# Adding attention's residual in TensorE's accumulator, and copying the sum with ScalarE

## The chip, the cores and the metric

The kernel runs on one core of one Trainium2 chip. The metric is device time in microseconds (us), the median of several runs. One more execution is recorded by the hardware profiler; its time and its span stand in the table below. The engines are TensorE (PE in the rows, PEld for its weight loads), VectorE (DVE), ScalarE (ACT), GpSimd (POOL) and SyncE (SP, which only issues transfers here). Each engine has its own list of instructions and works it off in order; engines meet through semaphores only.

## The reference

Sixteen sequences of 256 tokens with 128 features pass through half a mixture-of-experts block, an attention block, and half a mixture-of-experts block again. What the change touches is the middle line:

```
x = x + 0.5 * ffn(layernorm(x))
x = x + attn(layernorm(x))
x = x + 0.5 * ffn(layernorm(x))

def attn(x):                      # x here is layernorm(x), "xn" in the kernel
    q, k, v = split(einsum(rms_norm(x), w_qkv))
    q, k = rms_norm(q), rms_norm(k)
    w = exp(k); kv = w * v
    y = sigmoid(q) * cumsum(kv) / (cumsum(w) + 1e-6)
    u, g = split(einsum(y, w_swiglu))
    return x + einsum(u * silu(g), w_out)
```

So attention's new x is the old x, plus its layernorm xn, plus the projection of u * silu(g) with w_out.

## The kernel before

Tokens lie on 128 partitions; a tile is 128 tokens, X holds all 32 tiles in SBUF as [128, 32, 128] in fp32. The first and the last third of the time are the two mixture-of-experts layers (l = 0 and l = 1). Between them, from about 299 to 419 us, lies the attention stage, and the change lies wholly in it.

Attention works on one sequence at a time (two tiles, TB = 2; 16 sequences, BATCHES). It is cut into small stages, and each engine runs a software pipeline over them that is written out in full: in step k it runs, for each stage in the order of its list (POOL_STAGES, DVE_STAGES, ACT_STAGES, PE_STAGES), the stage for sequence k - lag, where the lag is the number beside the stage's name. Step k runs from 0 to 24. A stage begins with its waits on semaphores; an engine that waits there runs nothing of what stands behind.

One sequence goes through these stages (engine, lag; the names of the tiles are those of the rows):

- add_routed (POOL, 1): adds two loaded tiles Y to X. at_statistics and at_aggregate (DVE, 2 and 3), at_rsqrt and mean_square (POOL, 3 and 4), at_normalise (DVE, 4): the layernorm, written to xn.
- transpose_xn (PE, 4) into psT, copy_anT (ACT, 4) to anT, qkv (PE, 4) into psG or psH, squares (ACT, 4), qkv_rsqrt (POOL, 5: at_ms, then at_fac), weights (ACT, 5: wkv by Exp, tq by Tanh), weigh_v (DVE, 5).
- cumulate (PE, 6) into psU: three matmuls, of which the first and the third are lines 1643 and 1645. denominator (ACT, 6: den), invert, scale_q and attend (DVE, 6: rec, ysc, ya).
- transpose_y (PE, 7) into psT, copy_yT (ACT, 7) to yT, swiglu (PE, 7) into psU, tanh_g (ACT, 8: tg), gate_g and gate_u (DVE, 8: ag, ha).
- project (PE, 9) into psY, add_attention (DVE, 9): X = X + 0.5 * psY.
- residual (POOL, 5): X = X + xn, ahead of add_attention.

Waits that matter below: cumulate waits for attend of the sequence before it; transpose_xn waits for the copy_yT of the same step, since both use the psum tile psT; project waits for gate_u, and for the addition of the sequence before it to have read psY; gate_g waits for tanh_g.

From step 16 on, VectorE also begins the next layer's layernorm (stats and normalise, lines 761 to 774) of the chunks of four tiles that are done; LN_STEPS says in which step. From step 20 on, TensorE also transposes and scores these chunks (turn_chunk, score_chunk) at the head of a step.

Of the kernel before, what the change touches and what calls it, by code (L numbers as in the profile page):

```python
# [13 lines left out]
P = 128  # L14
D = 128
# [6 lines left out]
CH = 4  # L22
# [3 lines left out]
TB = SEQ // P  # L26
# [13 lines left out]
RING = 3  # L40
SEND_LAG = RING + 2
BATCH = 4
DEEP = 4
BATCHES_P = TOPK * TILES // BATCH
ROW = D + TOPK
# [24 lines left out]
SUM_LAG = 1  # L70

POOL_STAGES = [("qkv_rsqrt", 5), ("residual", 5), ("at_rsqrt", 3), ("mean_square", 4), ("add_routed", 1)]
DVE_STAGES = [("at_normalise", 4), ("at_aggregate", 3), ("gate_g", 8), ("at_statistics", 2), ("gate_u", 8),
              ("invert", 6), ("scale_q", 6), ("weigh_v", 5), ("attend", 6), ("add_attention", 9)]
ACT_STAGES = [("tanh_g", 8), ("denominator", 6), ("copy_yT", 7), ("copy_anT", 4),
              ("weights", 5), ("squares", 4)]
PE_STAGES = [("cumulate", 6), ("transpose_y", 7), ("project", 9), ("transpose_xn", 4), ("qkv", 4),
             ("swiglu", 7)]
# [1 line left out]

LN_STEPS = {}
for c in range(CHUNKS - 1):
    added = CH // TB * (c + 1) + dict(DVE_STAGES)["add_attention"]
# [11 lines left out]
fp32 = mybir.dt.float32  # L96
# [3 lines left out]
ALU = mybir.AluOpType  # L100
ACT = mybir.ActivationFunctionType
# [65 lines left out]
def macaron(nc, x, w_qkvT, w_swigluT, w_outT, gateT, w1_e, w3_e, w2_e, w1_s, w3_s, w2_s, out):  # L167
    ctx = ExitStack()
    with ctx:
# [6 lines left out]
        def sem(name):  # L176
            return ctx.enter_context(nc.semaphore(name))
# [6 lines left out]
        def overlaid(*groups):  # L184
# [7 lines left out]
            for name, shape, dt in groups[-1]:  # L192
# [3 lines left out]
        X = sb("X", [P, TILES, D])  # L196
# [13 lines left out]
        WOUT = sb("WOUT", [P, D])  # L210

        ident = sb("ident", [P, P])
# [47 lines left out]
        at_mv = sb("at_mv", [P, 2, TB, 2])  # L260
# [55 lines left out]
        pair = memory["pair"]  # L316

        memory = overlaid(
            [("xn", [P, 2, TB, D], fp32),
             ("anT", [P, 2, TB * P], fp32),  # L320
             ("sq", [P, 2, TB, D], bf16),
             ("wkv", [P, 2, TB, 2, D], fp32),
# [17 lines left out]
        xn = memory["xn"]  # L340
# [11 lines left out]
        ha = memory["ha"]  # L352
# [9 lines left out]
        psT = ps("psT", [P, 512])  # L362
        psY = ps("psY", [P, 512])
# [5 lines left out]
        attn_in = sem("attn_in")  # L369
# [71 lines left out]
        xres_done = sem("xres_done")  # L441
        anT_psum = sem("anT_psum")
        anT_done = sem("anT_done")
        qkv_psum = sem("qkv_psum")
# [14 lines left out]
        ha_done = sem("ha_done")  # L459
        at_psum = sem("at_psum")  # L460
        at_added = sem("at_added")

        psQKV = [psG, psH]
# [115 lines left out]
        def _(pool):  # L580
# [51 lines left out]
            for l in range(2):  # L632
# [77 lines left out]
                def residual(s):  # L710

                    wait_apart(pool, xn_ready, s.i + 1)
                    xs = X[:, bass.ds(s.i * TB, TB), :]
                    pool.tensor_tensor(xs, xs, xn[:, s.u % 2, :, :], ALU.add).then_inc(xres_done, 1)

                def qkv_rsqrt(s):

                    pool.wait_ge(ss_done, s.i + 1)
# [8 lines left out]
                                       .rearrange("p (a t) -> p a t", a=3), ALU.pow).then_inc(qk_scaled, 1)  # L727

                if l == 0:
                    stages = {"qkv_rsqrt": qkv_rsqrt, "add_routed": add_routed, "residual": residual,  # L730
                              "at_rsqrt": at_rsqrt, "mean_square": mean_square}
# [12 lines left out]
        def _(dve):  # L744
# [34 lines left out]
            for l in range(2):  # L779
# [332 lines left out]
                def at_normalise(s):  # L1112

                    dve.wait_ge(at_scaled, s.i + 1)
                    if s.past(2):
                        dve.wait_ge(anT_psum, s.i - 1)
                        dve.wait_ge(xres_done, s.i - 1)
                    for t in range(TB):
                        xt = X[:, bass.ds(s.i * TB + t, 1), :].rearrange("p a d -> p (a d)")
                        i = dve.tensor_scalar(xn[:, s.u, t, :], xt, at_mv[:, s.u, t, 0:1],  # L1120
                                              at_rstd[:, s.u, t:t + 1], ALU.subtract, ALU.mult)
                    i.then_inc(xn_ready, 1)

# [37 lines left out]
                    dve.tensor_tensor(ha[:, s.u, :], ag[:, s.u, :], psU[:, 1, 0:256], ALU.mult)\  # L1161
                       .then_inc(ha_done, 1)

                def add_attention(s):
                    dve.wait_ge(at_psum, s.i + 1)
                    dve.wait_ge(xres_done, s.i + 1)
                    xs = X[:, bass.ds(s.i * TB, TB), :].rearrange("p t d -> p (t d)")
                    dve.scalar_tensor_tensor(xs, psY[:, 0:TB * D], 0.5, xs, ALU.mult, ALU.add)\
                       .then_inc(at_added, 1)

                stages = {"weigh_v": weigh_v, "gate_u": gate_u, "add_attention": add_attention,
                          "at_normalise": at_normalise, "at_statistics": at_statistics, "attend": attend,
                          "at_aggregate": at_aggregate, "invert": invert, "scale_q": scale_q, "gate_g": gate_g}

# [13 lines left out]
        def _(act):  # L1188
            act.wait_ge(consts, CONSTS)
            for l in range(2):  # L1190
# [116 lines left out]
                if l == 1:  # L1307
                    continue

                def copy_anT(s):  # L1310
                    act.wait_ge(anT_psum, s.i + 1)
                    if s.past(2):
                        act.wait_ge(qkv_psum, s.i - 1)
                    act.activation(anT[:, s.u % 2, :], psT[:, 0:TB * P], ACT.Copy).then_inc(anT_done, 1)
# [44 lines left out]
                stages = {"copy_yT": copy_yT, "tanh_g": tanh_g, "weights": weights, "copy_anT": copy_anT,  # L1359
                          "squares": squares, "denominator": denominator}  # L1360
                def copy_turned(c):

# [25 lines left out]
        def _(pe):  # L1388
# [19 lines left out]
            for l in range(2):  # L1408
# [23 lines left out]
                for c in range(TURNED if l else 0, CHUNKS + 1):  # L1432
                    if c < CHUNKS:
# [5 lines left out]
                        for t in range(CH):  # L1439
                            i = pe.transpose(psH[:, c % 2, t * P:(t + 1) * P], XN[:, c * CH + t, 0:D], ident[:, :])  # L1440
# [176 lines left out]
                def transpose_xn(s):  # L1617
                    pe.wait_ge(xn_ready, s.i + 1)
                    issued = s.i + ((1 if y_first else 0) - apart)
                    if not isinstance(issued, int) or issued > 0:  # L1620
                        pe.wait_ge(yT_done, issued)
                    if s.past(1):
                        pe.wait_ge(anT_done, s.i)
                    for t in range(TB):
                        i = pe.transpose(psT[:, t * P:(t + 1) * P], xn[:, s.u, t, :], ident[:, :])
                    i.then_inc(anT_psum, 1)

                def qkv(s):
# [41 lines left out]
                def project(s):  # L1670
                    pe.wait_ge(ha_done, s.i + 1)
                    if s.past(1):
                        pe.wait_ge(at_added, s.i)
                    for t in range(TB):
                        i = pe.matmul(psY[:, t * D:(t + 1) * D], ha[:, s.u, t * P:(t + 1) * P], WOUT[:, :],
                                      start=True, stop=True)
                    i.then_inc(at_psum, 1)

                stages = {"project": project, "transpose_y": transpose_y, "swiglu": swiglu, "cumulate": cumulate,
# [70 lines left out]
```

## Time and profile before

| | |
|---|---|
| time, median of 3 runs | 709.31 us (708.37 to 711.33) |
| the profiled execution | 708.63 us, its span 706.9 us |
| busy over the span | PE 632.6, DVE 440.8, POOL 401.6, ACT 375.0 us |
| attention stage | about 299 to 419 us |

The span is the time from the first to the last instruction; 1.7 us lie around it. Busy shares over the whole span say little, since attention is a stage of its own with its own limits: it has to be read from stretches, and within a stretch from the order of instructions on each engine. A timeline row reads: start, length, engine, line, operation, out<-in, tile shape, and how many instructions were merged into it (x2); in brackets, how long the engine sat idle before, and which instruction of another engine ended that. An fp32 matmul shows as two records, a transpose as one, so project's two matmuls are "x4".

### The profile page before, as it was taken

All of it is one profiled execution on the core that took longest, in us unless ns stands there. A gap on an engine that the chain in (4) does not pass through costs nothing.

```text
span 706.9 us, 13752 instructions
## 1 busy us (share of the span) xinstructions
PE 632.6 (89%) x4622; PEld 572.5 (81%) x4622; DVE 440.8 (62%) x1167; ACT 375.0 (53%) x819; POOL 401.6 (57%) x485
## 2 busy tenths in 40 slices
PE   3877998999999999858886777899999999999995
PEld 2656888999999999725664574788999999999983
DVE  6679785555445553359999876975545554455336
ACT  2657725666666652146664536572666666665220
POOL 5610065677777773479987416005577777777330
PEclk9999999999999999979999997799999999999999
DMA  9634011223332121221100000701222332222137
GB/s 295 251 63 60 1 32 43 72 84 86 111 83 51 53 53 62 87 75 45 46 16 1 0 1 1 122 0 32 47 75 82 111 84 81 54 53 54 57 125 260
DMA packets 38820, 51.38 MB, mean 73 GB/s; under 512 B 6432, under 2 KB 27936, under 8 KB 38368
## 3 DMA queue, kind: packets, MB, share of 16 engines
q1 hardware_dynamic: 29664, 31.73, 15.5%
q0 software_dynamic: 9088, 18.78, 10.3%
q8 instruction: 39, 0.64, 0.4%
q14 instruction: 29, 0.24, 0.1%
HBM read 34.81 MB, written 15.66 MB: 71 GB/s over the span
## 4 chain that ended last, share of the span: by engine, by line
PE 64%; DVE 20%; issue 4%; POOL 4%; ACT 4%; DMA 3%; SPq 1%; POOLq 0%; ACTq 0%; DVEq 0%
PE psY L1573 17%; PE psU L1394 5%; PE psG L1394 5%; PE psU L1395 5%; PE psU L1396 5%; PE psH L1467 5%; PE psG L1395 5%; PE psG L1396 5%; DVE rec L1136 3%; PE psT L1495 2%; DVE XN L774 2%; DVE hs L784 2%; PE psU L1525 2%; PE psG L1525 2%; DVE ln_stats L761 1%
## 5 line engine op out<-in xcount | busy, mean ns | idle before, releaser
L662 POOL DMA_INDIRECT rows<-tokens,source x142 | 138.9, 978 | 156.6 <-DVE source L955 101.3
L1215 ACT ACTIVATE silu<-psG 128x512 f32<-128x512 f32 x206 | 122.7, 596 | 170.5 <-PE psG L1396 130.6
L1014 DVE TENSOR_TENSOR hT<-silu,psU 128x512 f32<-128x512 f32 x142 | 97.5, 687 | 151.9 <-PE psU L1396 122.8
L677 POOL DMA_INDIRECT results<-yout,target x142 | 139.6, 983 | 64.0 <-issue 41.5
L1573 PE MATMUL psY<-W,hT 128*128 x1104 | 145.5, 275 | 0.0
L1573 PEld LDWEIGHTS psY<-W,hT 128*128 128x128 f32 x1104 | 134.6, 191 | 0.2 <-DVE hT L1014 0.2
L1289 ACT ACTIVATE w_high<-W13H 128x1024 fp32r x64 | 67.8, 1060 | 48.1 <-PE psU L1396 43.4
L1394 PE MATMUL psG<-xTH,w_high 128*128 128x256 f32 x256 | 82.4, 322 | 0.7 <-ACT w_low L1289 0.7
L1395 PE MATMUL psG<-xTL,w_high 128*128 128x256 f32 x256 | 71.6, 280 | 0.0
L1396 PE MATMUL psG<-xTH,w_low 128*128 128x256 f32 x256 | 71.6, 280 | 0.0
L1395 PE MATMUL psU<-xTL,w_high 128*128 128x256 f32 x256 | 71.5, 279 | 0.0
L1394 PE MATMUL psU<-xTH,w_high 128*128 128x256 f32 x256 | 71.5, 279 | 0.0
L1396 PE MATMUL psU<-xTH,w_low 128*128 128x256 f32 x256 | 71.5, 279 | 0.0
L784 DVE TENSOR_TENSOR hs<-silu,psU 128x512 f32<-128x512 f32 x64 | 43.6, 683 | 38.0 <-PE psU L1396 30.2
L1289 ACT ACTIVATE w_low<-W13L 128x1024 fp32r x64 | 67.1, 1048 | 0.0
L1467 PEld LDWEIGHTS psH<-W2S,hs 128*128 128x128 f32 x512 | 60.4, 195 | 5.8 <-DVE hs L784 4.7
L1467 PE MATMUL psH<-W2S,hs 128*128 128x128 f32 x512 | 61.1, 278 | 2.9 <-DVE hs L784 2.9
L1394 PEld LDWEIGHTS psG<-xTH,w_high 128*128 128x128 f32 x256 | 48.6, 190 | 0.9 <-issue 0.9
L1395 PEld LDWEIGHTS psG<-xTL,w_high 128*128 128x128 f32 x256 | 48.6, 190 | 0.0
L1394 PEld LDWEIGHTS psU<-xTH,w_high 128*128 128x128 f32 x256 | 48.1, 188 | 0.0
L1395 PEld LDWEIGHTS psU<-xTL,w_high 128*128 128x128 f32 x256 | 48.0, 188 | 0.0
L1396 PEld LDWEIGHTS psG<-xTH,w_low 128*128 128x128 f32 x256 | 48.0, 188 | 0.0
(212 smaller groups left out, 1250.7 us busy)
## 6 DMA issues: line engine op xcount, KB each, us to landing
w_single<-w_e SPq DMA_DIRECT2D x28, 256.0 KB, 3.1
W<-w_e SPq DMA_DIRECT2D x3, 2048.0 KB, 13.8
tokens<-XN SPq DMA_DIRECT2D x16, 260.0 KB, 6.5
Y<-results SPq DMA_DIRECT2D x32, 128.0 KB, 2.2
YF<-results SPq DMA_DIRECT2D x16, 256.0 KB, 5.7
rows<-tokens,source POOLq DMA_INDIRECT x142
results<-yout,target POOLq DMA_INDIRECT x142, 2.3
X<-x SPq DMA_DIRECT2D x8, 256.0 KB, 5.5
```

Of the source, the lines that this page charges most:

```text
L662: pool.indirect_dma_start(rows[:, slot(l, g), t, :], None, tokens, bass.IndirectOffsetOnAxis(ap=source[:, tile:tile + 1], axis=0))\
L677: pool.indirect_dma_start(results, bass.IndirectOffsetOnAxis(ap=target[:, tile:tile + 1], axis=0), yout[:, g % 2, t, :], None).then_inc(y_ ...
L784: dve.tensor_tensor(hidden, silu[:, turn % 2, :], psU[:, turn % 2, :], ALU.mult).then_inc(h_done, 1)
L1014: dve.tensor_tensor(hT[:, s.u // PT % 2, half, :].rearrange("p f c -> p (f c)"), silu[:, turn % 2, :], psU[:, turn % 2, :], ALU.mult).then ...
L1215: act.activation(silu[:, turn % 2, :], psG[:, turn % 2, :], ACT.Silu).then_inc(silu_done, 1)
L1289: act.activation(used[p % 2][:, :, :], kept[:, :, bass.ds(entries[p], F)], ACT.Copy)\
L1394: pe.matmul(out, a_high, b_high, start=True, stop=False)
L1395: pe.matmul(out, a_high, b_low, start=False, stop=False)
L1396: return pe.matmul(out, a_low, b_high, start=False, stop=True)
L1467: i = pe.matmul(psH[:, par, t * D:(t + 1) * D], hs[:, par, f, t * P:(t + 1) * P], W2S[:, f, :], start=(f == 0), stop=(f == FT - 1))
L1525: i = pe.matmul(out[:, turn % 2, f * P:(f + 1) * P], w_single[:, n % SINGLE_HOMES, w, f * P:(f + 1) * P], xT_whole[:, par, t, :], start=Tr ...
L1573: i = pe.matmul(into[:, t * D:(t + 1) * D], h, W2[:, bass.ds(at + f * D, D)], start=(f == 0), stop=(f == FT - 1))
```

## The change

The addition of xn to X on GpSimd (residual) and the addition of the projection to X on VectorE (add_attention) are gone. Project instead runs three matmuls for each of the two tiles into the same part of psY: X with the identity matrix, xn with the identity matrix, and ha with WOUT; WOUT is multiplied by 0.5 once, on ScalarE, ahead of the first step. A new stage, keep_sum, with lag 9 on ScalarE, copies psY to X. It stands first in ScalarE's list. Since xn must now live until project reads it, it has seven buffers where it had two, and at_normalise waits for the project of seven sequences ago.

```
-POOL_STAGES = [("qkv_rsqrt", 5), ("residual", 5), ("at_rsqrt", 3), ("mean_square", 4), ("add_routed", 1)]
+POOL_STAGES = [("qkv_rsqrt", 5), ("at_rsqrt", 3), ("mean_square", 4), ("add_routed", 1)]
...
-              ("invert", 6), ("scale_q", 6), ("weigh_v", 5), ("attend", 6), ("add_attention", 9)]
-ACT_STAGES = [("tanh_g", 8), ("denominator", 6), ("copy_yT", 7), ("copy_anT", 4),
+              ("invert", 6), ("scale_q", 6), ("weigh_v", 5), ("attend", 6)]
+ACT_STAGES = [("keep_sum", 9), ("tanh_g", 8), ("denominator", 6), ("copy_yT", 7), ("copy_anT", 4),
...
                 def at_normalise(s):
                     dve.wait_ge(at_scaled, s.i + 1)
-                    if s.past(2):
-                        dve.wait_ge(anT_psum, s.i - 1)
-                        dve.wait_ge(xres_done, s.i - 1)
+                    if s.past(XN_RING):
+                        dve.wait_ge(at_psum, s.i - XN_RING + 1)
...
-                def add_attention(s):
-                    dve.wait_ge(at_psum, s.i + 1)
-                    dve.wait_ge(xres_done, s.i + 1)
-                    xs = X[:, bass.ds(s.i * TB, TB), :].rearrange("p t d -> p (t d)")
-                    dve.scalar_tensor_tensor(xs, psY[:, 0:TB * D], 0.5, xs, ALU.mult, ALU.add)\
-                       .then_inc(at_added, 1)
...
+                act.wait_ge(attn_in, 48)
+                act.activation(WOUT[:, :], WOUT[:, :], ACT.Copy, scale=0.5).then_inc(wout_halved, 1)
+
+                def keep_sum(s):
+                    act.wait_ge(at_psum, s.i + 1)
+                    act.activation(X[:, s.i * TB:(s.i + 1) * TB, :].rearrange("p t d -> p (t d)"), psY[:, 0:TB * D],
+                                   ACT.Copy).then_inc(at_added, 1)
...
                 def project(s):
...
                     for t in range(TB):
-                        i = pe.matmul(psY[:, t * D:(t + 1) * D], ha[:, s.u, t * P:(t + 1) * P], WOUT[:, :],
-                                      start=True, stop=True)
+                        into = psY[:, t * D:(t + 1) * D]
+                        pe.matmul(into, ident[:, :], X[:, s.i * TB + t, :], start=True, stop=False)
+                        pe.matmul(into, ident[:, :], xn[:, s.i % XN_RING, t, :], start=False, stop=False)
+                        i = pe.matmul(into, ha[:, s.u, t * P:(t + 1) * P], WOUT[:, :], start=False, stop=True)
                     i.then_inc(at_psum, 1)
```

On ScalarE, one step of the middle of the stage, from squares of one step to weights of the next, before (tg is tanh_g, den denominator; behind each row the semaphores that it waits for):

```order
L1323 ACTIVATE sq,qk_ss<-psH 128x128 x3
L1357 ACTIVATE tg<-psU 128x256 [waits uv_psum]
L1346 ACTIVATE den<-psU 128x256 [waits ya_done,cum_psum]
L1353 ACTIVATE yT<-psT 128x256 [waits uv_psum,yT_psum]
L1314 ACTIVATE anT<-psT 128x256 [waits qkv_psum,anT_psum]
L1333 ACTIVATE wkv<-psH,at_fac 128x128 [waits ya_done,qk_scaled]
```

and the same place with the change (line numbers are a few lower in the changed file):

```order
L1318 ACTIVATE sq,qk_ss<-psH 128x128 x3
L1302 ACTIVATE X<-psY 128x256 [waits at_psum]
L1352 ACTIVATE tg<-psU 128x256 [waits uv_psum]
L1341 ACTIVATE den<-psU 128x256 [waits ya_done,cum_psum]
L1348 ACTIVATE yT<-psT 128x256 [waits uv_psum,yT_psum]
L1309 ACTIVATE anT<-psT 128x256 [waits qkv_psum,anT_psum]
```

The copy of psY, with a wait for project, now stands between the squares and tanh_g. On TensorE, from cumulate to transpose_xn of one step, before:

```order
L1643 MATMUL psU<-wkv,upto 128x256 [waits ya_done,kv_done]
L1644 MATMUL psU<-wkv,ones 128x256
L1645 MATMUL psU<-wkv,upto 128x256
L1657 MATMUL psT<-ident,ya 128x128 [waits yT_done,anT_done,ya_done]
L1675 MATMUL psY<-WOUT,ha 128x128 [waits at_added,ha_done]
L1625 MATMUL psT<-ident,xn 128x128 [waits anT_done,yT_done,xn_ready]
```

and with the change, the transposes and both tiles' matmuls written once each:

```order
L1640 MATMUL psU<-wkv,upto 128x256
L1652 MATMUL psT<-ident,ya 128x128 [waits yT_done,anT_done,ya_done]
L1673 MATMUL psY<-X,ident 128x128 [waits at_added,ha_done]
L1674 MATMUL psY<-xn,ident 128x128
L1675 MATMUL psY<-WOUT,ha 128x128
L1620 MATMUL psT<-ident,xn 128x128 [waits anT_done,yT_done,xn_ready]
```

Project keeps its place, behind cumulate and transpose_y and ahead of transpose_xn, and has six matmuls for two.

## Rows read from the trace of the kernel before

**Rows 1.** Busy time by stretch: us, then PE, PEld, DVE, ACT, POOL; clock, DMA, GB/s.

```profile
340.00:360.00 20.00, 18.06 (x86) 13.27 (x84) 19.76 (x64) 12.53 (x59) 18.49 (x32) 1.00 0.14 41
...
380.00:400.00 20.00, 13.60 (x60) 9.25 (x61) 19.59 (x68) 10.13 (x46) 12.34 (x25) 1.00 0.00 1
```

**Rows 2.** Groups of instructions, 300 to 430 us: busy, mean ns | idle before.

```profile
L714 POOL TENSOR_TENSOR X<-X,xn 128x256 f32<-128x256 f32 x16 | 11.6, 724 | 0.0
...
L1675 PE MATMUL psY<-WOUT,ha 128*128 128x128 f32 x64 | 9.8, 275 | 0.0
...
L1168 DVE SCALAR_TENSOR_TENSOR X<-psY,X 128x256 f32<-128x256 f32 x16 | 6.7, 417 | 1.6 <-PE psY L1675 1.6
```

**Rows 3.** Timeline of VectorE in step 11: gate_g, and attend.

```profile
342.32 0.41 DVE L1154 SCALAR_TENSOR_TENSOR ag<-tg,psU 128x256 f32<-128x256 f32 x1
...
346.01 0.41 DVE L1148 TENSOR_TENSOR ya<-ysc,psU 128x256 f32<-128x256 f32 x1
```

**Rows 4.** Timeline of TensorE: cumulate, transpose_xn, the next cumulate.

```profile
341.25 0.66 PE L1643 MATMUL psU<-wkv,upto 128*128 128x256 f32 x2
...
342.19 0.59 PE L1645 MATMUL psU<-wkv,upto 128*128 128x256 f32 x2
...
343.58 0.41 PE L1625 MATMUL psT<-ident,xn 128*128 128x128 f32 x2
...
346.72 0.59 PE L1643 MATMUL psU<-wkv,upto 128*128 128x256 f32 x2
```

**Rows 5.** Timeline of GpSimd (at_fac) and ScalarE in the same step.

```profile
342.12 1.33 POOL L726 TENSOR_TENSOR at_fac<-at_ms,minus_half 128x6 f32<-128x6 f32 x1
...
342.82 0.38 ACT L1346 ACTIVATE den<-psU 128x256 f32<-128x256 f32 x1 [0.81 <-PE psU L1645]
343.10 0.38 ACT L1353 ACTIVATE yT<-psT 128x256 f32<-128x256 f32 x1
344.02 0.38 ACT L1314 ACTIVATE anT<-psT 128x256 f32<-128x256 f32 x1 [0.55 <-PE psT L1625]
344.30 0.62 ACT L1333 ACTIVATE wkv<-psG,at_fac 128x128 f32<-128x128 f32 x2
```

**Rows 6.** Timeline at step 19, where cumulate waits for attend; project.

```profile
392.00 0.41 DVE L1148 TENSOR_TENSOR ya<-ysc,psU 128x256 f32<-128x256 f32 x1
...
392.56 0.67 PE L1643 MATMUL psU<-wkv,upto 128*128 128x256 f32 x2 [0.93 <-DVE ya L1148]
...
394.15 0.61 PE L1675 MATMUL psY<-WOUT,ha 128*128 128x128 f32 x4
```

**Rows 7.** Timeline of VectorE in step 16: two chunks' layernorm, later gate_g.

```profile
368.44 0.86 DVE L761 BATCH_NORM_STATS2 ln_stats<-X 128x6 f32<-128x128 f32 x4
...
373.18 0.41 DVE L1154 SCALAR_TENSOR_TENSOR ag<-tg,psU 128x256 f32<-128x256 f32 x1
```

**Rows 8.** Timeline of the first steps: qkv_rsqrt on GpSimd, the end of squares.

```profile
309.42 0.20 POOL L723 TENSOR_TENSOR at_ms<-qk_ss,at_eps 128x4 f32<-128x4 f32 x1 [2.05 <-ACT sq L1323]
...
324.33 0.22 ACT L1323 ACTIVATION_READ_ACCUMULATOR sq<-psH 128x1 f32 x1
...
325.93 0.20 POOL L723 TENSOR_TENSOR at_ms<-qk_ss,at_eps 128x4 f32<-128x4 f32 x1
```

**Rows 9.** Timeline: cumulate of steps 9 and 21, and the last chunk's statistics.

```profile
329.93 0.67 PE L1643 MATMUL psU<-wkv,upto 128*128 128x256 f32 x2
...
406.47 0.60 PE L1643 MATMUL psU<-wkv,upto 128*128 128x256 f32 x2
...
418.75 0.87 DVE L761 BATCH_NORM_STATS2 ln_stats<-X 128x6 f32<-128x128 f32 x4
```

**Rows 10.** A long gap on TensorE, and the clock (before DMA) of its stretch.

```profile
372.90 0.44 PE L1625 MATMUL psT<-ident,xn 128*128 128x128 f32 x2 [2.29 <-DVE xn L1120]
...
372.00:376.00 4.00, 2.63 (x6) 1.45 (x7) 3.94 (x13) 1.52 (x5) 3.77 (x8) 0.79 0.02 4
```

**Rows 11.** Chain that ended last: matmuls with the identity, 512 columns wide.

```profile
697.15 1.72 PE psT L1594 x4
```

More of the change, by code:

```diff
@@ L42 @@
 BATCH = 4
+XN_RING = 7
 DEEP = 4
@@ L83 @@
 for c in range(CHUNKS - 1):
-    added = CH // TB * (c + 1) + dict(DVE_STAGES)["add_attention"]
+    added = CH // TB * (c + 1) + dict(ACT_STAGES)["keep_sum"]
     LN_STEPS.setdefault(max(BATCHES + max(c - 1, 0), added), []).append(c)
@@ L318, in macaron @@
         memory = overlaid(
-            [("xn", [P, 2, TB, D], fp32),
+            [("xn", [P, XN_RING, TB, D], fp32),
              ("anT", [P, 2, TB * P], fp32),
@@ L440, in macaron @@
         xn_ready = sem("xn_ready")
-        xres_done = sem("xres_done")
         anT_psum = sem("anT_psum")
@@ L461, in macaron @@
         at_added = sem("at_added")
+        wout_halved = sem("wout_halved")
         psQKV = [psG, psH]
@@ L708, in mean_square @@
                                        rms_eps[:, :, :], ALU.mult).then_inc(rms_terms, 1)
[L710 to L714, printed above, removed]
                 def qkv_rsqrt(s):
@@ L729, in _ @@
                 if l == 0:
-                    stages = {"qkv_rsqrt": qkv_rsqrt, "add_routed": add_routed, "residual": residual,
-                              "at_rsqrt": at_rsqrt, "mean_square": mean_square}
+                    stages = {"qkv_rsqrt": qkv_rsqrt, "add_routed": add_routed, "at_rsqrt": at_rsqrt, "mean_square": mean_square}
                     def scale_ahead(chunks):
@@ L1114, in at_normalise @@
                     dve.wait_ge(at_scaled, s.i + 1)
-                    if s.past(2):
-                        dve.wait_ge(anT_psum, s.i - 1)
-                        dve.wait_ge(xres_done, s.i - 1)
+                    if s.past(XN_RING):
+                        dve.wait_ge(at_psum, s.i - XN_RING + 1)
                     for t in range(TB):
                         xt = X[:, bass.ds(s.i * TB + t, 1), :].rearrange("p a d -> p (a d)")
-                        i = dve.tensor_scalar(xn[:, s.u, t, :], xt, at_mv[:, s.u, t, 0:1],
+                        i = dve.tensor_scalar(xn[:, s.i % XN_RING, t, :], xt, at_mv[:, s.u, t, 0:1],
                                               at_rstd[:, s.u, t:t + 1], ALU.subtract, ALU.mult)
@@ L1162, in gate_u @@
                        .then_inc(ha_done, 1)
-                def add_attention(s):
-                    dve.wait_ge(at_psum, s.i + 1)
-                    dve.wait_ge(xres_done, s.i + 1)
-                    xs = X[:, bass.ds(s.i * TB, TB), :].rearrange("p t d -> p (t d)")
-                    dve.scalar_tensor_tensor(xs, psY[:, 0:TB * D], 0.5, xs, ALU.mult, ALU.add)\
-                       .then_inc(at_added, 1)
-                stages = {"weigh_v": weigh_v, "gate_u": gate_u, "add_attention": add_attention,
+                stages = {"weigh_v": weigh_v, "gate_u": gate_u,
                           "at_normalise": at_normalise, "at_statistics": at_statistics, "attend": attend,
@@ L1357, in tanh_g @@
                     act.activation(tg[:, s.u % 2, :], psU[:, 1, 256:512], ACT.Tanh, scale=0.5).then_inc(tg_done, 1)
-                stages = {"copy_yT": copy_yT, "tanh_g": tanh_g, "weights": weights, "copy_anT": copy_anT,
+                stages = {"keep_sum": keep_sum, "copy_yT": copy_yT, "tanh_g": tanh_g, "weights": weights, "copy_anT": copy_anT,
                           "squares": squares, "denominator": denominator}
@@ L1624, in transpose_xn @@
                     for t in range(TB):
-                        i = pe.transpose(psT[:, t * P:(t + 1) * P], xn[:, s.u, t, :], ident[:, :])
+                        i = pe.transpose(psT[:, t * P:(t + 1) * P], xn[:, s.i % XN_RING, t, :], ident[:, :])
                     i.then_inc(anT_psum, 1)
@@ L1673, in project @@
                         pe.wait_ge(at_added, s.i)
+                    if s.i == 0:
+                        pe.wait_ge(wout_halved, 1)
                     for t in range(TB):
-                        i = pe.matmul(psY[:, t * D:(t + 1) * D], ha[:, s.u, t * P:(t + 1) * P], WOUT[:, :],
-                                      start=True, stop=True)
+                        into = psY[:, t * D:(t + 1) * D]
+                        pe.matmul(into, ident[:, :], X[:, s.i * TB + t, :], start=True, stop=False)
+                        pe.matmul(into, ident[:, :], xn[:, s.i % XN_RING, t, :], start=False, stop=False)
+                        i = pe.matmul(into, ha[:, s.u, t * P:(t + 1) * P], WOUT[:, :], start=False, stop=True)
                     i.then_inc(at_psum, 1)
```

## The prediction

> **What bounds the stage now.** I read the busy time by stretch first. In the middle of attention VectorE is busy 19.76 of 20 us and GpSimd 18.49; TensorE has 18.06; ScalarE has room, 12.53 [rows 1]. So VectorE sets the pace there. In the later stretch, with the next layernorm on VectorE too, it has 19.59 of 20 and TensorE falls to 13.60. The groups then say what VectorE and GpSimd would be rid of: add_attention, 16 times 417 ns, 6.7 us, and residual, 16 times 724 ns [rows 2]. If nothing else happened, that would be a gain.
>
> The timelines say what hangs on what. Take step 11 with cumulate's first matmul (line 1643) as zero, at 341.25; the next step's is at 346.72, so a step lasts 5.47 us [rows 4]. The step's VectorE chain from gate_g (342.32) to the end of attend (346.01 + 0.41) is 4.10 us long [rows 3], and the next cumulate needs that attend: where it waited for it, it began 0.15 after its end (392.00 + 0.41 to 392.56) [rows 6]. Now look at what feeds gate_g. Tanh_g needs only swiglu of the step before, and ScalarE runs it right behind the squares, before cumulate has ended: ScalarE then sits idle 0.81 us until cumulate gives it den's input [rows 5]. So VectorE's chain starts before TensorE's part of the step is through, and the two lie side by side.
>
> **The change, part by part.** *What project costs.* Two fp32 matmuls are four records in 0.61 us, of which one alone takes 0.275 [rows 2, 6]; each further record adds (0.61 - 0.275) / 3 = 0.112. The trace of before has matmuls with the identity: four records, two matmuls of 512 columns, in 1.72, or 0.43 / 4 = 0.108 for each record's 128 columns [rows 11]. So the identity is no cheaper than a weight. A transpose of the same shape is one record instead of two; that is the lower bound, half the price. I take the matmul's. Four more matmuls are 8 x 0.112 = 0.90 us a step, and project lasts 11 x 0.112 + 0.275 = 1.51 from its first record to its last result.
>
> *What keep_sum costs.* A copy of this shape from psum takes 0.38 and the next instruction starts 0.28 after it (342.82 to 343.10) [rows 5]. That is the small part. Its wait is the large one: at the head of ScalarE's step stands an instruction that needs project of the same step, and behind it stand tanh_g, den, yT, anT. Rows 5 show how such a wait works: at_fac was there at 342.12 + 1.33 = 343.45, and ScalarE idled until 344.02 for anT, and only then, at 344.30, ran wkv, whose input it had.
>
> *The new step.* From cumulate at 0: project begins at 1.59 (392.56 to 394.15) [rows 6] and ends at 3.10. ScalarE follows a psum result by 0.04 (342.19 + 0.59 to 342.82) [rows 4, 5]: keep_sum 3.14, tanh_g 3.42, done with the length of a copy, 0.38, at 3.80. With the same 0.04, gate_g starts at 3.84, attend ends 4.10 later at 7.94, and the next cumulate begins 0.15 after, at 8.09. This is a ring: attend, cumulate, transpose_y, project, keep_sum, tanh_g, gate_g, attend. Nothing in it overlaps with anything else in it, and it holds for each step from 9, the first with a project, on. The way through TensorE is shorter: den follows tanh_g, yT starts at 4.02 to 4.10, ends 0.38 later, transpose_xn 0.10 after that (343.10 + 0.38 to 343.58) at 4.50 to 4.58, and from there to the next cumulate it is 3.14 (343.58 to 346.72) [rows 4]; together 7.6 to 7.7. So 8.09 binds, and VectorE and TensorE both have idle time in it.
>
> *What is hidden.* In the new ring VectorE waits for tanh_g from about -0.15 (attend's end) to 3.84 of each step, 3.99. That hides at_normalise, at_aggregate and one chunk's layernorm, which made the later steps long before. With two chunks, in step 16, it is too little: from the layernorm's start to gate_g it was 373.18 - 368.44 = 4.74 [rows 7], 0.75 over; with one chunk it is well under. The halving of WOUT is one small instruction ahead of ScalarE's first step, where it has nothing to do; at an activation's 0.4 it would cost no more if it had. The ring of seven xn buffers waits for a project two steps back, which is done. VectorE's own work of a step, 5.47 - 0.4 in the middle, is under 8.09, so it binds only if the ring is shorter than I think.
>
> *Before step 9*, when there is no project, the change helps. GpSimd sets the pace of steps 5 to 8: three steps from 309.42 to 325.93, 5.50 each; and at 325.93 the squares had been ready since 324.33 + 0.22 = 324.55, 1.38 earlier [rows 8]. The loop from at_fac over squares to at_fac spans two steps, so 0.69 a step can be won, just about residual's length. Three to four steps: 2.1 to 2.8. I take 2.4.
>
> *The sum.* Steps 9 to 21 of before: 406.47 - 329.93 = 76.5 us for 12 steps [rows 9]. After: 12 x 8.09 = 97.1, plus 0.75 for step 16, plus about 1.1 because steps 20 and 21 have transposes and scores ahead of cumulate (in 21, twelve records, 1.3, begun a little before attend ends): 98.9. That is 22.4 more. From cumulate of step 21 to the last chunk's statistics it was 12.28 (to 418.75) [rows 9]; there three more steps of swiglu, scores and project follow, each behind ScalarE's copy_yT, which now comes 4.50 - 2.33 = 2.17 later (2.33 is 341.25 to 343.58) [rows 4]: 6.5. Less 2.4 at the start: 26.5. The profiled execution took 708.63, so 735.1; it lies 0.7 under the median of the runs, and the steps without statistics (18 and later) are a few tenths shorter than I counted, so I leave it at **735**.
>
> **The rivals.** *The wait is hidden, the matmuls are not.* If tanh_g were not held up, a step would be TensorE's: 5.47 + 0.90 = 6.37 for the seven steps to 16, 6.3 more; the later steps would gain VectorE's 0.4 four times, 1.6; the last three would pay 0.9 each, 2.7; the start gives 2.4. Together 5 more: 714. Against it: ScalarE's order, and rows 5. It would need swiglu's tanh to be ahead of keep_sum, which it is not.
>
> *Faster.* VectorE is the bound and is rid of 6.7 us, GpSimd of 11.6, of which 2.4 count; ScalarE has room. That gives 708.6 - 9.1, about 700. For it speaks VectorE's 19.76 of 20 [rows 1]. It decides where gate_g is not later than before, that is, where tanh_g is done 1.1 after cumulate's start (342.32 - 341.25) [rows 3, 4]; project alone ends 2.0 after that. The Trainium skill, in "Perfetto Trace Analysis", section "Optimizing Scalar/DVE Operations", says that moving work to ScalarE may make sense where VectorE is saturated. It is saturated here, and by that rule the time would be this rival's; the rule counts busy time and not the order in which ScalarE waits.
>
> *TensorE's clock falls.* In before, a gap of 2.29 us on TensorE was followed by a stretch with a granted clock of 0.79, part of it at the lower of its two levels [rows 10]. A new step has 48 records' worth of 128 columns (cumulate 12, transposes 4, project 12, qkv 12, swiglu 8), 5.4 us of 8.1; at 1.2 GHz it takes 5.4 more. If six of the 15 steps fell, some 25 to 30 us would come on top: about 763. Against it: the longest new gap, from project's last record (1.59 + 12 x 0.112 = 2.93) to transpose_xn at 4.5, is 1.6; and TensorE busy 13.60 of 20, the same share as 5.4 of 8.1, went with a clock of 1.00 [rows 1]. The Trainium skill, in "TensorE: Matmul & The Clock Gate", section "A second HAM failure mode: psum-queue depth-cycling", describes a kernel whose small idle times between groups of matmuls made the clock go up and down; by it the change would be worse than my sum. Rows 1 disagree for a stretch of this density.
>
> **Chances.** The ring as worked out 0.78; the clock 0.09; the wait hidden 0.05; faster 0.05; something unseen, near no change, 0.03. Terms that can be off: identity records at the price of a transpose, 15 x 0.45 = 7 less; the start without gain, 2.4 more; the tail 2 either way; a clock that falls in one or two steps, up to 10 more. So 727 to 747 holds the likeliest case, and with a chance of 0.78 and a part of the clock's it is the range. A difference of 0.5%, 3.5 us, is about what a measurement of this kernel can tell from none: faster 0.05, same 0.03, slower 0.92.
>
> **What would show it.** In the profile after: in the middle of the stage VectorE's busy share falls from 99% to about 63% (5.07 of 8.09), and gate_g is the instruction it waits for, with tanh_g as the releaser and 2 to 3 us idle each step (less where a layernorm stands ahead). keep_sum waits for project each step. Transpose_xn waits about 1.5 us for copy_yT. Cumulates of steps 10 to 16 lie 8.1 apart, and those of 17 to 19 about the same, though layernorm work is added there. The first at_fac rows come 0.7 closer together. The stage ends about 26 us later, and what follows is unchanged. I would be wrong if cumulates were 6.4 apart (the wait is hidden), if project's six matmuls took 1.1 and not 1.5, or if TensorE's clock fell within the stage.

## The result, and the profile after

The changed kernel takes 747.84 us, the median of six runs (742.45 to 749.24); the kernel before, in the same rounds, 708.91 (708.37 to 711.33). The ratio is 1.053, with an interval of 1.0508 to 1.0553. That is 38.9 us slower where I forecast about 26 us, and 0.84 over the upper end of my range. The direction and the mechanism were right, the size was not. The profiled execution took 749.24, its span 747.4; it is the slowest of the six, against 708.63 and 706.9 before.

Busy time over the whole span (the page's first part) says that TensorE has more to do and VectorE and GpSimd less, which is true and explains nothing:

```profile
PE 660.5 (88%) x4750; PEld 596.9 (80%) x4750; DVE 435.5 (58%) x1151; ACT 379.3 (51%) x836; POOL 388.7 (52%) x469
```

The same two stretches as in [rows 1] (columns as there, the granted clock third from the end):

```profile
340.00:360.00 20.00, 14.71 (x73) 11.06 (x71) 10.58 (x33) 8.76 (x38) 10.84 (x23) 0.91 0.09 27
380.00:400.00 20.00, 16.03 (x69) 11.72 (x68) 15.51 (x64) 8.80 (x42) 10.49 (x18) 0.86 0.00 1
```

VectorE, 19.76 of 20 us before, is at 10.58. Every engine has idle time, so no engine is the bound any more: a chain through TensorE, ScalarE and VectorE is. And the clock, 1.00 before, is 0.91 and 0.86. The list of waits, 300 to 465 us (engine, line, the engine and line waited for; total, times, longest), names the two instructions in which the chain waits:

```profile
ACT X L1302 <- PE psY L1675: 60.2, 16, 8.5
...
DVE ag L1147 <- ACT tg L1352: 45.8, 15, 6.2
```

Keep_sum waits for project 16 times of 16, and gate_g for tanh_g 15 times. One step, in the timeline, with only the rows of the chain:

```profile
330.25 0.67 PE L1638 MATMUL psU<-wkv,upto 128*128 128x256 f32 x2
...
331.84 0.39 PE L1673 MATMUL psY<-X,ident 128*128 128x128 f32 x2
...
332.96 0.39 PE L1675 MATMUL psY<-WOUT,ha 128*128 128x128 f32 x2
...
333.38 0.38 ACT L1302 ACTIVATE X<-psY 128x256 f32<-128x256 f32 x1 [2.77 <-PE psY L1675]
...
333.66 0.38 ACT L1352 ACTIVATE tg<-psU 128x256 f32<-128x256 f32 x1
...
334.07 0.42 DVE L1147 SCALAR_TENSOR_TENSOR ag<-tg,psU 128x256 f32<-128x256 f32 x1 [3.02 <-ACT tg L1352]
...
334.69 0.41 PE L1620 MATMUL psT<-ident,xn 128*128 128x128 f32 x2 [1.35 <-issue]
...
337.77 0.41 DVE L1141 TENSOR_TENSOR ya<-ysc,psU 128x256 f32<-128x256 f32 x1
...
338.32 0.67 PE L1638 MATMUL psU<-wkv,upto 128*128 128x256 f32 x2 [0.33 <-DVE ya L1141]
```

Counted from cumulate: project 1.59 to 3.10, keep_sum 3.13, tanh_g 3.41 to 3.79, gate_g 3.82, attend's end 7.93, the next cumulate 8.07. The prediction had 1.59, 3.10, 3.14, 3.42, 3.80, 3.84, 7.94 and 8.09. This is an undisturbed step. Every second one is not. Here are qkv and swiglu of this step, of the next, and qkv of a later one:

```profile
335.58 1.56 PE L1628 MATMUL psH<-WQKV,anT 128*128 128x384 f32 x4 [0.47 <-ACT anT L1309]
336.97 1.03 PE L1661 MATMUL psU<-yT,WSW 128*128 128x256 f32 x4
...
343.64 2.09 PE L1628 MATMUL psG<-WQKV,anT 128*128 128x384 f32 x4 [0.47 <-ACT anT L1309]
345.53 1.91 PE L1661 MATMUL psU<-yT,WSW 128*128 128x256 f32 x4
347.23 0.95 PE L1638 MATMUL psU<-wkv,upto 128*128 128x256 f32 x2
...
412.72 2.88 PE L1628 MATMUL psG<-WQKV,anT 128*128 128x384 f32 x4 [0.47 <-ACT anT L1309]
```

The same instructions take 2.09 and 1.91 instead of 1.56 and 1.03, nothing waits in between, and the window over them has a granted clock of 0.57, where 1.00 is 2.4 GHz and 0.50 the lower level of 1.2:

```profile
344.00:348.00 4.00, 4.00 (x10) 2.74 (x9) 3.15 (x11) 1.77 (x11) 0.93 (x2) 0.57 0.20 60
```

The cumulates of steps 9 to 16 lie 8.07, 8.91, 8.36, 9.11, 8.16, 9.27 and 8.00 us apart: two steps take 17.27 together instead of 16.14. TensorE's clock, the rival to which I gave 0.09, came on top of the ring.

### The profile page after: what moved, and what is told of

It reads as the page before. It is cut to its first block, busy times and chain, and to the rows that moved or that the text cites. A ratio compares the mean times of both kernels' runs of the same rounds, so it can differ in the third digit from the quotient of the medians.

```text
span 747.4 us, 13973 instructions
## 1 busy us (share of the span) xinstructions
PE 660.5 (88%) x4750; PEld 596.9 (80%) x4750; DVE 435.5 (58%) x1151; ACT 379.3 (51%) x836; POOL 388.7 (52%) x469
## 4 chain that ended last, share of the span: by engine, by line
PE 71%; DVE 13%; issue 5%; ACT 5%; DMA 3%; POOL 2%; SPq 1%; ACTq 0%; POOLq 0%; DVEq 0%
PE psY L1568 16%; PE psH L1462 5%; PE psG L1389 5%; PE psU L1389 5%; PE psU L1390 5%; PE psU L1391 5%; PE psG L1390 5%; PE psG L1391 5%; PE psG L1628 2%; PE psT L1490 2%; DVE rec L1129 2%; PE psU L1661 2%; DVE hs L778 1%; PE psG L1520 1%; PE psU L1520 1%
```

## Where the 40.5 us of the span went

The end of the stretches in after, as in [rows 9]: cumulate of step 21, swiglu in the next step, and the last chunk's statistics.

```profile
436.83 1.06 PE L1638 MATMUL psU<-wkv,upto 128*128 128x256 f32 x2
...
443.21 1.10 PE L1661 MATMUL psU<-yT,WSW 128*128 128x256 f32 x4 [1.75 <-DVE ha L1154]
...
458.23 0.87 DVE L755 BATCH_NORM_STATS2 ln_stats<-X 128x6 f32<-128x128 f32 x4 [3.02 <-ACT X L1302]
```

| stretch | before | forecast | after | more |
|---|---|---|---|---|
| start of the span to cumulate of step 9 | 329.93 | 327.5 | 330.25 | +0.3 |
| cumulate 9 to cumulate 21 | 76.54 | 98.9 | 106.58 | +30.0 |
| cumulate 21 to the last statistics | 12.28 | 18.8 | 21.40 | +9.1 |
| the rest of the span | 288.15 | 288.15 | 289.17 | +1.0 |

Three terms are off: 7.7 us in the steps, 2.7 at the start, 2.6 in the tail. The experiments take them, and the rivals, one by one. Each kernel was timed beside the kernel before (medians of 708.25, 708.59 and 708.87 in the three batches).

## Experiments on the ring

**ScalarE's order alone.** The changed kernel with keep_sum moved in ScalarE's list, first behind copy_yT, then behind tanh_g only:

```diff
-ACT_STAGES = [("keep_sum", 9), ("tanh_g", 8), ("denominator", 6), ("copy_yT", 7), ("copy_anT", 4),
+ACT_STAGES = [("tanh_g", 8), ("denominator", 6), ("copy_yT", 7), ("keep_sum", 9), ("copy_anT", 4),
```
```diff
-ACT_STAGES = [("keep_sum", 9), ("tanh_g", 8), ("denominator", 6), ("copy_yT", 7), ("copy_anT", 4),
+ACT_STAGES = [("tanh_g", 8), ("keep_sum", 9), ("denominator", 6), ("copy_yT", 7), ("copy_anT", 4),
```

> The changed kernel with keep_sum moved in ScalarE's list from the first place to behind copy_yT, nothing else. Theory (the order makes a ring through keep_sum and tanh_g): the ring is gone, a middle step falls from 8.07 to what TensorE needs, 5.47 + 0.9 or about 6.3; time about 716 us (712 to 720). Rival (the four added matmuls are what costs): they are all still there, so the time stays within 5 us of the changed kernel's 748.

> The changed kernel with keep_sum behind tanh_g and ahead of den. Theory: tanh_g no longer waits for project, but den and yT still do. The ring through gate_g is shorter than the way through TensorE: project ends 3.10 after cumulate, keep_sum 3.14, den 3.42, yT 3.70 to 4.08, transpose_xn 4.18, next cumulate 3.14 later, 7.3 a step; 12 steps at 0.75 less than 8.07 give about 739, a little less if the clock falls less often. Rival (only tanh_g's delay counts): as with keep_sum behind yT, about 716.

Behind copy_yT: 713.21 us, ratio 1.0069 (1.0046 to 1.0092), 6.02 a step. Behind tanh_g: 729.49, 1.0296 (1.0267 to 1.0326), 7.23 a step. The same instructions, the same matmuls: the change costs 5.0 us where it cost 38.9, by the place of one copy in one list (some 8 of these 34 us are falls of the clock, priced below, which do not come in this order: no window from 316 to 432 us has less than 1.00). The timeline of the first, from cumulate at 341.05 to the next at 347.08:

```profile
341.41 0.40 ACT L1352 ACTIVATE tg<-psU 128x256 f32<-128x256 f32 x1
...
343.91 0.38 PE L1620 MATMUL psT<-ident,xn 128*128 128x128 f32 x2
344.11 0.38 ACT L1302 ACTIVATE X<-psY 128x256 f32<-128x256 f32 x1 [0.90 <-PE psY L1675]
344.39 0.38 ACT L1309 ACTIVATE anT<-psT 128x256 f32<-128x256 f32 x1
```

Tanh_g starts 0.36 after cumulate instead of 3.41. Keep_sum still waits, but only copy_anT is behind it, and transpose_xn follows project with no gap, since copy_yT is long done. I expected 6.3 a step for that order; it is 6.02, because in my 5.47 + 0.90 the transpose still waited for copy_yT, and here project fills that wait. The second order was expected near 739 and came out at 729; its step is as worked out (7.23 for 7.3), and what I had added for falls of the clock did not come: no window from 316 to 440 us has less than 1.00.

**The wait alone.** The kernel before, with a copy of a weight tile within SBUF to a spare tile at the head of ScalarE's list, that waits for project. Both additions stay where they were; the copied tile is not used.

```diff
-ACT_STAGES = [("tanh_g", 8), ("denominator", 6), ("copy_yT", 7), ("copy_anT", 4),
+ACT_STAGES = [("copy_sum", 9), ("tanh_g", 8), ("denominator", 6), ("copy_yT", 7), ("copy_anT", 4),
...
+                def copy_sum(s):
+                    act.wait_ge(at_psum, s.i + 1)
+                    act.activation(spare[:, :], WSW[:, :], ACT.Copy)
```

> The kernel before, with one thing added: at the head of ScalarE's list a stage that waits for project (lag 9) and then copies a weight tile of 256 columns within SBUF to a spare tile that nobody reads. No matmul is added, VectorE and GpSimd keep both additions. The theory of the ring (the wait ahead of tanh_g is the cost): project, now two matmuls, ends 1.59 + 0.61 = 2.20 after cumulate's first matmul, the copy starts at 2.24, tanh_g at 2.52, done at 2.90, gate_g at 2.94, attend ends 4.10 later, the next cumulate 0.15 after that: a step of about 7.2 us in the middle where before has 5.47. Seven steps of 1.7 and a tail of 4 to 6: about 725 (720 to 732), and more if TensorE's clock falls. The rival (the four identity matmuls are the cost, the wait is covered): the steps stay near 5.5 and the time near 709.

730.11 us, ratio 1.0304 (1.0273 to 1.0334), inside the expected range, and 7.20 a step (7.19 worked out) where the clock stays up. Here too it falls, twice in the stage: the granted clock is 0.68 from 356 to 360 us and 0.57 from 388 to 392, and the first fall makes steps 12 and 13 last 15.54 together instead of 14.40. Its timeline has the same two waits as after's, 2.26 and 1.83, though no work was moved between engines (the cumulates around it at 344.87 and 352.07):

```profile
347.10 0.42 ACT L1314 ACTIVATE spare<-WSW 128x256 f32<-128x256 f32 x1 [2.26 <-PE psY L1681]
...
347.82 0.42 DVE L1155 SCALAR_TENSOR_TENSOR ag<-tg,psU 128x256 f32<-128x256 f32 x1 [1.83 <-ACT tg L1363]
```

**The matmuls alone.** The kernel before, with four matmuls of the identity with itself added to project; their results are not used.

```diff
                     for t in range(TB):
+                        for _ in range(2):
+                            pe.matmul(psY[:, 256:384], ident[:, :], ident[:, :], start=True, stop=True)
```

> The kernel before, with four matmuls of the identity with itself added to each project, into a part of psY that nobody reads; the additions stay where they are and ScalarE's list is as before. If the matmuls are only TensorE's time, the middle step goes from 5.47 to between 6.0 and 6.4 (0.90 more by the sum, less what TensorE sat idle), and the time to 714 to 717. The rival (the matmuls are the main cost of the change): steps near 8 and a time near 740.

715.57 us, ratio 1.0078 (1.0053 to 1.0103), 5.97 a step: 0.50 more than before's 5.47, the rest of 0.90 falls into idle time of TensorE. So the wait alone costs 21.5 us, its two falls of the clock included, the matmuls alone 7.0; in the ring the matmuls add their whole length (8.07 - 7.20 = 0.87), since project lies in it.

## Experiments on the clock

**Work in the idle time behind project, then elsewhere.** The changed kernel with unused matmuls of the identity with itself in steps 9 to 19: six behind project; two behind project; the same two elsewhere, one behind transpose_xn and one behind swiglu (this one a step later, ahead of the cumulates of steps 11 to 20). But for the last step or two, all stand where TensorE otherwise waits.

```diff
                     i.then_inc(at_psum, 1)
+                    if s.i <= 10:
+                        for _ in range(6):
+                            pe.matmul(psQKV[1 - s.u][:, 0, 0:P], ident[:, :], ident[:, :], start=True, stop=True)
```

The second kernel has range(2) there. The third has instead, at the end of transpose_xn and at the head of cumulate:

```diff
+                    if 5 <= s.i <= 15:
+                        pe.matmul(psQKV[s.u][:, 0, 0:P], ident[:, :], ident[:, :], start=True, stop=True)
...
+                    if 5 <= s.i <= 14:
+                        pe.wait_ge(at_added, s.i - 3)
+                        pe.matmul(psY[:, 256:384], ident[:, :], ident[:, :], start=True, stop=True)
```

> The changed kernel with six more fp32 matmuls of the identity (twelve records, 1.34 us, results unused) behind project of sequences 0 to 10, in a psum bank that is free then, so that they lie in TensorE's 1.57 us gap before transpose_xn. Clock theory (the falls in every second step come from idle time): the clock stays at 1.00 from step 9 to 19, all steps take 8.07 instead of 8.07 and 9.27 in turn, five or six falls of 1.1 are gone: about 741. Rival (the clock's falls have another cause, or TensorE's work is the cost): 748 or more, with the same alternation.

> The changed kernel with two matmuls of the identity with itself (0.45 us) right behind project, in steps 9 to 19, into a psum part that nobody reads. They stand in TensorE's longest idle time of the step, 1.35 us between project and transpose_xn, and cut it to about 0.9. If the clock falls because of the length of that one idle time, no step of 9 to 19 shows a lower clock, each lasts 8.07, and the time is about 741, as with six matmuls there (740.4). If it is the amount of work that counts, two are a third of six, and this kernel and the one with the same two matmuls elsewhere show the same number of falls; between 741 and 748.

> The changed kernel with the same two matmuls in the same steps, but in the two short idle times: one behind transpose_xn, where TensorE waits 0.47 us for ScalarE's anT, and one behind swiglu, where it waits 0.33 for attend. The idle time of 1.35 between project and transpose_xn stays. If its length makes the clock fall, the falls stay in every second step and the time is about 748 (745 to 750); if the amount of work counts, the falls go, or become as few as with the two matmuls behind project.

| | us | ratio (interval) | steps 9 to 16, each |
|---|---|---|---|
| six behind project | 740.43 | 1.0453 (1.0429 to 1.0478) | 8.00 to 8.07 |
| two behind project | 739.33 | 1.0441 (1.0412 to 1.0469) | 8.07 or 8.08 |
| two elsewhere | 741.2 | 1.0468 (1.0443 to 1.0494) | 8.00 to 8.08 |
| none (after) | 747.84 | 1.053 (1.0508 to 1.0553) | 8.00 to 9.27 |

More work on TensorE makes the kernel 6.6 to 8.5 us faster. In the third kernel the idle time behind project is as long as in after, and the clock stays up all the same. In the timeline, and in the window 340 to 380 us of that kernel:

```profile
344.23 0.41 PE L1620 MATMUL psT<-ident,xn 128*128 128x128 f32 x2 [1.35 <-issue]
344.48 0.39 PE L1623 MATMUL psG<-ident 128*128 128x128 f32 x2
```
```profile
340.00:380.00 40.00, 31.58 (x170) 24.84 (x169) 24.54 (x75) 18.69 (x85) 20.63 (x40) 1.00 0.07 21
```

and in after:

```profile
340.00:380.00 40.00, 30.23 (x139) 22.16 (x138) 23.25 (x67) 17.72 (x77) 19.29 (x39) 0.90 0.07 21
```

So the theory that the length of this one gap makes the clock fall is out; 0.45 us more work in a step, and as much less idle time, ended the falls in either place. The expectation of 748 for this kernel was wrong, its other branch right. Behind the last of these matmuls, in step 20, the first and the third kernel fall once (0.58 and 0.60 from 428 to 432 us). The kernel with two matmuls behind project has a granted clock of 1.00 in every 4-us window from 312 us to the end of the stage; it is the changed kernel without falls, and its rows give the terms of the sum by themselves:

```profile
428.63 0.60 PE L1638 MATMUL psU<-wkv,upto 128*128 128x256 f32 x2
...
433.40 1.10 PE L1661 MATMUL psU<-yT,WSW 128*128 128x256 f32 x4 [1.75 <-DVE ha L1154]
```
```profile
448.43 0.87 DVE L755 BATCH_NORM_STATS2 ln_stats<-X 128x6 f32<-128x128 f32 x4 [3.02 <-ACT X L1302]
```

With its cumulate of step 9 at 330.21, steps 9 to 21 take 98.42 (98.9 forecast), and the tail 19.80.

## Experiments on the start, and on the faster rival

**Residual left out.** The kernel before without GpSimd's addition of xn (its output lacks that term), and nothing in its place:

```diff
-POOL_STAGES = [("qkv_rsqrt", 5), ("residual", 5), ("at_rsqrt", 3), ("mean_square", 4), ("add_routed", 1)]
+POOL_STAGES = [("qkv_rsqrt", 5), ("at_rsqrt", 3), ("mean_square", 4), ("add_routed", 1)]
```

> The kernel before without GpSimd's addition of xn (its output lacks that term); nothing takes its place. By the prediction's term for the start, cumulate of step 9 comes 2.1 to 2.8 us earlier, and the total by about 2.4 us or more: 706 or less. The rival, from the trace of after: the squares are late next, and then VectorE's chain from den to attend, and VectorE's normalise and scale take longer since GpSimd's additions of Y now fall on them; cumulate of step 9 then moves by less than 0.6 us, and the total stays at 708 to 709.

708.5 us, ratio 0.999 (0.9975 to 1.0004): no difference, as the rival says. From cumulate of step 6 to that of step 9 it takes 16.88 us, after 16.87, before 17.02: 0.05 a step won, not 0.69. In its timeline GpSimd now waits:

```profile
325.67 0.22 POOL L716 TENSOR_TENSOR at_ms<-qk_ss,at_eps 128x4 f32<-128x4 f32 x1 [1.84 <-ACT sq L1314]
```

and after shows what is late next, two ways from one cumulate to the next: TensorE's own, with its waits for ScalarE's copies, and the one over ScalarE's den and VectorE's rec, ysc and ya. The rows are TensorE's for one such step, and VectorE's for this step, with ysc of the step before, and for the next:

```profile
319.27 0.67 PE L1638 MATMUL psU<-wkv,upto 128*128 128x256 f32 x2 [1.83 <-DVE ya L1141]
...
321.60 0.41 PE L1620 MATMUL psT<-ident,xn 128*128 128x128 f32 x2 [0.57 <-issue]
...
323.88 1.03 PE L1661 MATMUL psU<-yT,WSW 128*128 128x256 f32 x4
324.74 0.59 PE L1638 MATMUL psU<-wkv,upto 128*128 128x256 f32 x2
```
```profile
317.38 0.90 DVE L1133 SCALAR_TENSOR_TENSOR ysc<-tq,rec 128x256 f32<-128x256 f32 x1
...
321.26 1.75 DVE L1129 RECIPROCAL rec<-den 128x256 f32<-128x256 f32 x1 [0.80 <-ACT den L1341]
323.05 0.53 DVE L1133 SCALAR_TENSOR_TENSOR ysc<-tq,rec 128x256 f32<-128x256 f32 x1
...
324.02 0.41 DVE L1141 TENSOR_TENSOR ya<-ysc,psU 128x256 f32<-128x256 f32 x1
...
328.44 0.82 DVE L1133 SCALAR_TENSOR_TENSOR ysc<-tq,rec 128x256 f32<-128x256 f32 x1
...
329.70 0.40 DVE L1141 TENSOR_TENSOR ya<-ysc,psU 128x256 f32<-128x256 f32 x1
```

The cumulate at 324.74 stands right behind swiglu, 0.31 after the end of ya: TensorE's way held it, 5.47 long. The next, at 330.25, begins 0.15 after the end of ya: VectorE's way held it, 5.51 long. Both are just under the 5.67 of before, and VectorE's has become longer itself: ysc takes 0.53 to 0.90 in these steps, 0.42 in before. GpSimd, rid of residual, now runs its additions of Y beside it; in before they began behind ya, beside instructions that are not on this way:

```profile
317.28 0.72 POOL L629 TENSOR_TENSOR X<-X,Y 128x256 f32<-128x256 f32 x1
318.08 0.78 POOL L631 TENSOR_TENSOR X<-X,Y 128x256 f32<-128x256 f32 x1
```

**VectorE relieved, without the wait.** The kernel before with add_attention gone: X, with xn added by GpSimd as before, is put into psY by one 256-column matmul with the identity behind transpose_xn, project adds to it with the halved WOUT, and keep_sum stands behind copy_yT.

```diff
+                def start_sum(s):
+                    pe.wait_ge(xres_done, s.i + 1)
...
+                    pe.matmul(psY[:, 0:TB * D], ident[:, :],
+                              X[:, s.i * TB:(s.i + 1) * TB, :].rearrange("p t d -> p (t d)"), start=True, stop=False)
```

> Built on the kernel before: GpSimd adds xn to X as before (residual stays), but X then goes into psY by one identity matmul of 256 columns for each sequence, placed behind transpose_xn, where TensorE waits 0.47 for anT; project adds ha with the halved WOUT to it; ScalarE copies psY to X behind copy_yT. VectorE is rid of add_attention. Theory (order decides): TensorE's step stays about 5.3 to 5.4 since the identity lies in its gap, VectorE's falls from 5.47 to 5.1: 0.1 less in each of 7 middle steps, 0.3 to 0.4 in each of 5 steps with layernorm, the last steps lose a little: about 706 (703 to 710). Rival (any identity matmul on TensorE costs more than VectorE gains): 711 to 715.

709.97 us, ratio 1.0032 (1.0017 to 1.0046): 4 us above the expected 706, and still 5.47 a step in the middle. VectorE has one instruction less, and another one longer; xn, and the two additions on GpSimd beside it:

```profile
345.69 1.13 DVE L1121 TENSOR_SCALAR xn<-X,at_mv,at_rstd 128x128 f32<-128x128 f32 x2
```
```profile
344.94 0.72 POOL L629 TENSOR_TENSOR X<-X,Y 128x256 f32<-128x256 f32 x1
345.74 0.72 POOL L631 TENSOR_TENSOR X<-X,Y 128x256 f32<-128x256 f32 x1
```

Xn takes 1.13 for the 0.63 and 0.78 that it takes in the same stretch of before, which eats the 0.4. The Trainium skill, in "SBUF — State Buffer", section "Who interferes with whom", says that GpSimd's only ports are also VectorE's second pair, and that a VectorE instruction with two SBUF inputs, or a tensor_scalar in a faster mode, waits there for GpSimd or holds it up. The rows agree for ysc (two inputs in SBUF, 0.42 to 0.90) and xn (a tensor_scalar, 0.63 to 1.13); no run here isolates the port.

VectorE's 0.4 was worth little in these steps anyway. TensorE's own way is 5.39 in this kernel, from cumulate at 340.59 to the next, which stands right behind swiglu:

```profile
340.59 0.59 PE L1646 MATMUL psU<-wkv,upto 128*128 128x256 f32 x2
...
345.12 1.03 PE L1669 MATMUL psU<-yT,WSW 128*128 128x256 f32 x4
345.98 0.60 PE L1646 MATMUL psU<-wkv,upto 128*128 128x256 f32 x2
```

And what the stage gained it lost again. From cumulate of step 9 to that of step 21 it takes 74.70 us, 1.84 less than before; from there (404.35) to the last statistics 14.45, 2.17 more. In these last steps TensorE waits for ScalarE's copy of the sum before it can start the next one:

```profile
407.04 0.67 PE L1677 MATMUL psY<-X,ident 128*128 128x256 f32 x2 [0.56 <-ACT X L1310]
...
418.80 0.87 DVE L762 BATCH_NORM_STATS2 ln_stats<-X 128x6 f32<-128x128 f32 x4 [3.59 <-ACT X L1310]
```

## Why the prediction came out as it did

**The ring: right.** The order of the step, the two waits, and each time in it are within 0.02 us. The wait alone in the old kernel gives 7.20 where the same working gave 7.19, and taking keep_sum from the head of the list gives the time of my rival "the wait is hidden": 713.21 for the 714 that I had worked out. That one is partly luck: by its profile steps 9 to 21 cost 2.7 more and not 4.7, the last steps 3.8 and not 2.7, and cumulate of step 9 came 1.0 earlier and not 2.4, 0.84 of it from ahead of step 6. Six matmuls took 1.51, not 1.1. Two chunks of layernorm in step 16 cost 0.69 (8.76 in the kernel without falls; 0.75 forecast), and steps 20 and 21 together 1.1 (8.46 and 8.81; 1.1 forecast). VectorE's busy share from 340 to 360 us fell to 53%, not to 63; in the kernel with two matmuls behind project it is 59% there and 62% from 340 to 380.

**TensorE's clock: the step that failed.** I gave it 0.09 with two arguments. One was the longest gap, 1.6; it is 1.35, and the clock fell all the same, in every second step; and in the kernel with two matmuls elsewhere it did not fall with the same gap. The other was that TensorE's 13.60 of 20 us went with a clock of 1.00 in before; that one stretch stayed up says little about another with its work in other places. The falls cost 106.58 - 98.42 = 8.2 us in the steps and 21.40 - 19.80 = 1.6 in the tail by the profiles, and 747.84 - 739.33 = 8.5 by the medians. My price was for six fallen steps with all their matmuls at the lower level, 25 to 30 us; a fall covered only part of a step, and cost 1.13. The section of the Trainium skill that I set aside, "A second HAM failure mode: psum-queue depth-cycling" of "TensorE: Matmul & The Clock Gate", describes another kernel, whose small idle times between groups of matmuls make the clock go up and down: the trace agrees with it, at 0.57 in one window and 1.00 in those around it. The six runs fit: the one of 742.45 had a mean clock of 0.970, that of 749.24 one of 0.954.

**The start: a term of 2.4 that was 0.15.** (Cumulate of step 6 itself came 0.47 later in after, 313.38 for 312.91, which makes up the rest of the row above.) I saw that GpSimd waited for nothing and that the squares were 1.38 early, and took that for the room. I did not look for what is late next: TensorE's way and the one through den and attend are 5.47 and 5.51 long. That is the way to overrate the removal of a bound.

**The tail: 6.5 that was 7.5.** By the timeline of the kernel without falls the last two swiglu and the scores behind them are 2.2, 2.6 and 1.9 us later than in before, 6.7 in all, close to 3 x 2.17. The last project's four additional matmuls, 0.9, stand on the path to the last statistics too, and I had left them out. Swiglu there waits for gate_u (1.75) and not for copy_yT as I wrote: both hang on the late tanh_g, and the size came out the same.

With the start and the tail corrected, 735 becomes 738.4; the three kernels without falls in the middle take 739.3 to 741.2.

**Faster: wrong.** For VectorE at 99% I had said that relief would help if nothing else happened, and that VectorE sets the pace. But in the step that I took, attend ended at 346.42 and the next cumulate began at 346.72 [rows 3, 4], 0.30 later where 0.15 is enough [rows 6], and TensorE had no idle time ahead of it: its own way was as long as VectorE's work. So there was 0.1 a step to win and not 0.4. With the wait out of the way and VectorE relieved the step was still 5.47, with a longer xn on VectorE and TensorE's 5.39 just behind; the 1.8 us that the steps up to 21 did win went again in the last ones. The Trainium skill's advice in "Perfetto Trace Analysis", "Optimizing Scalar/DVE Operations", that moving work to ScalarE may make sense where VectorE is saturated, gained nothing here: 1.7 us more in the best order that I tried, 5.0 in the next, and 38.9 in the worst.

No version that keeps the whole sum beats the kernel before.

## What to carry to other kernels

When work moves to another engine, read that engine's list: what stands behind the moved instruction inherits its wait, and here the same change cost 5 us with the copy behind copy_yT and 39, falls of the clock included, with it at the head. Before counting a removed bound as gain, find the chain that is late next and its length, and see which of its instructions the relieved engine will now run beside. And when a step gets longer with TensorE idle in it, let the clock be a case with real weight, even if no gap is long; a few unused matmuls in the idle time show what it costs.

## What the runs showed of the hardware

I had not expected the clock to fall in a step whose longest idle time on TensorE is 1.35 us, nor that it would do so in alternation: a step of 8.07 at 1.00, then one with qkv and swiglu partly at the lower level, in pairs of 17.27 us, with qkv at 2.09 first and 2.88 four pairs later. Two more matmuls in a step, 0.45 us, ended it. The old kernel with the wait alone, with 1.37 as the longest idle time of its steps 9 to 15, fell once in them. Why before's long steps, with TensorE at 13.60 of 20 us, stay at 1.00 and these do not, no run here settles. The other thing is that VectorE's xn and ysc take up to about twice their time (1.13 for 0.6, 0.90 for 0.42) beside GpSimd's additions, so that time taken off one of these engines can come back on the other.
